# Three attentions turned round: scores by key tiles instead of by query tiles

## The reference

```python
q, k, v = x @ wq, x @ wk, x @ wv                       # [1250, 8, 64]; cross: q of one input, k and v of the other
att = softmax(einsum('bthd,bshd->bhts', q, k) * 64 ** -0.5, axis=-1)
o = einsum('bhts,bshd->bthd', att, v)                  # then an output projection
```

## Time and profile before

| | us |
|---|---|
| median of 3 runs (3291.41 to 3301.77) | 3301.08 |
| profiled execution, whole | 3298.01 |
| profiled execution, span of the instructions | 3296.2 |
| mean granted TensorE clock of the span | 0.949 |
| TensorE matmul busy, share of the span | 2932.8, 89% |
| VectorE busy | 2036.8, 62% |
| ScalarE busy | 1465.3, 44% |
| POOL busy | 940.6, 29% |

### The profile page before, as it was taken

How to read it: one execution, slowest core, us unless ns; L and a number is a source line. 1 busy time by engine, 2 the same in 40 slices (tenths; PEclk the granted TensorE clock), 3 DMA queues, 4 the chain that set the end, 5 groups by cost and what they waited for, 6 DMA issues and landing times. The chain is left out here.

```text
span 3296.2 us, 48091 instructions
## 1 busy us (share of the span) xinstructions
PE 2932.8 (89%) x15718; PEld 2060.1 (62%) x15718; DVE 2036.8 (62%) x4423; ACT 1465.3 (44%) x3160; POOL 940.6 (29%) x994
## 2 busy tenths in 40 slices
PE   5978789999679967699998888989999899998899
PEld 3522277776557644355555765668777687776787
DVE  7989745776421126599996355643777537776444
ACT  1000035666235425477774345533666336664322
POOL 2057663672124431577770000000000000001210
PEclk9999989999779979799999899999999899999999
DMA  3047665331559964554541554136320163311322
GB/s 99 14 134 205 193 165 144 63 61 38 168 164 339 338 195 142 199 154 146 159 122 42 176 132 104 26 107 185 68 59 22 44 189 81 73 25 40 105 83 83
DMA packets 222610, 402.73 MB, mean 122 GB/s; under 512 B 44222, under 2 KB 140626, under 8 KB 218526
## 3 DMA queue, kind: packets, MB, share of 16 engines
q1 hardware_dynamic: 170866, 262.09, 28.0%
q0 software_dynamic: 49744, 134.92, 14.7%
q10 hardware_dynamic: 1756, 2.64, 0.3%
HBM read 315.84 MB, written 87.71 MB: 122 GB/s over the span
## 5 line engine op out<-in xcount | busy, mean ns | idle before, releaser
L904 ACT ACTIVATE at_p<-at_pb,at_max 125x1250 f32<-125x1250 f32 (+4 forms) x320 | 383.8, 1199 | 301.3 <-DVE at_unused L975 272.9
L790 PE MATMUL at_pb<-ident,at_p 125*125 125x125 f32 x2880 | 435.2, 282 | 20.2 <-ACT at_p L904 17.4
L790 PEld LDWEIGHTS at_pb<-ident,at_p 125*125 125x125 f32 x2880 | 392.3, 191 | 82.6 <-ACT at_p L904 23.4
L807 PE MATMUL at_pb<-at_pt,at_v 125*64 125x250 f32 x2880 | 355.3, 383 | 5.2 <-DVE s_t L1008 3.0
L968 DVE TENSOR_REDUCE at_wide<-at_pb 125x1 f32<-125x1024 f32 x240 | 293.6, 1224 | 22.4 <-PE at_pb L773 4.5
L890 ACT ACTIVATE at_pt<-at_pb 125x500 f32<-125x500 f32 (+1 forms) x448 | 232.8, 520 | 97.5 <-PE at_pb L790 93.7
L807 PEld LDWEIGHTS at_pb<-at_pt,at_v 125*64 125x64 f32 x2880 | 188.4, 137 | 103.9 <-issue 13.8
L750 PE MATMUL at_pb<-at_s,at_shared 128*128 128x500 f32 (+1 forms) x1152 | 229.4, 361 | 24.0 <-ACT at_shared L852 24.0
L986 DVE COPY at_pt<-at_pb 125x500 f32<-125x500 f32 (+1 forms) x416 | 232.5, 582 | 22.4 <-PE at_pb L790 22.4
L975 DVE TENSOR_SCALAR_CACHE_REDUCE at_unused<-at_pb,at_wide 125x226 bf16<-125x226 f32 x240 | 107.7, 449 | 205.1 <-PE at_pb L773 202.2
L750 PEld LDWEIGHTS at_pb<-at_s,at_shared 128*128 128x128 f32 x1152 | 195.9, 194 | 57.1 <-ACT at_shared L852 24.7
(11 more groups left out here) (336 smaller groups left out, 5709.2 us busy)
## 6 DMA issues: line engine op xcount, KB each, us to landing
w_ring<-in_L_ffn_w SPq DMA_DIRECT2D x128, 512.0 KB, 12.2
at_shared<-k_parts SPq DMA_DIRECT2D x64, 312.5 KB
ml_w<-in_mlp_w SPq DMA_DIRECT2D x64, 256.0 KB
k_parts<-at_shared SPq DMA_DIRECT2D x64, 250.0 KB, 2.8
q_parts<-at_shared SPq DMA_DIRECT2D x64, 250.0 KB, 3.2
h_edges<-em_both SPq DMA_DIRECT2D x11, 1024.0 KB, 4.1
g_h<-h_edges SPq DMA_DIRECT2D x11, 1024.0 KB, 6.4
at_shared<-q_parts SPq DMA_DIRECT2D x32, 312.5 KB
```

Source lines behind the costliest of these rows:

```text
L790: ins = pe.transpose(pturn[0:TN, g % 2, TN * (t % 4):TN * (t % 4) + TN], p[:, u % 2, TN * t:TN * t + TN], c.ident[0:TN, 0:TN])
L807: ins = pe.matmul(pout[side:side + 64, 0:2 * TN], v[:, t, 2 * j + h, :], p_t[:, q % 2, t, :], start=(t < 2), stop=(t >= keys[u] - 2))
L904: act.activation(p[:, t % 2, 0:w], score[t % 2][0:TN, 0:w], ACT.Exp, bias=neg_max[:, t:t + 1], accum_out=total[:, t:t + 1]).then_inc(exp_d ...
```

## The change

A new function, `attention_by_key`, takes the place of `attention` in the three unmasked attentions; the causal one keeps the old function. The scores are made transposed, 125 keys on the partitions by queries on the columns, so that the exponentials are already in the form that the weighted sum takes and nothing is transposed.

- A *pass* is one head and one half of the queries (16 passes). Its ten *steps* are the key tiles; the half is two chunks of 312 (or 316) columns in two PSUM banks. Two steps are a *stretch* (`u`).
- A step has four score matmuls: high q and low q (stacked on 128 partitions) against high k, then 65 rows: high q against low k, and one row that holds the negative maximum of each query against a row of ones. So the maximum is subtracted by TensorE, and ScalarE's exponential has no bias.
- The maxima come from matmuls of their own, by query tiles of 125 and key pieces of 418 and 416 columns, of the high part of k alone: 15 a pass, three a stretch, in two banks (4 and 5) that the row sums share. VectorE reduces each; the last one of a pass is followed by a small reduction, and SP writes the pass's five columns of maxima as pieces of the row, by five DMAs. The maxima of a pass run six to two stretches ahead of it, those of the first 18 during the v projection.
- The weighted sum: for each step two fp32 matmuls (chunk 0 to partitions 0 to 63, chunk 1 to 64 to 127), summed over ten steps in one of two banks.
- Row sums: POOL adds up the exponentials of some key tiles (five in four additions; three in two in layer 0), VectorE those of the others, and four matmuls with a matrix of ones sum over the partitions. ScalarE copies the sums, spreads a row of 316 over 79 partitions by four by DMA, VectorE inverts them 8 wide, ScalarE sends them to DRAM and spreads them over 64 partitions, and POOL (layer 0: VectorE) multiplies `out_t` in SBUF. The last pass is inverted 316 wide from PSUM and multiplied by VectorE.
- Projections run in the order q, k, v, and SP instead of POOL issues the first pair's loads, in the middle of the second half of k (its q in the second half of q).

```diff
+QUARTERS = ((0, 312), (618, 316))
+MOSTQ = 316
+MAX_CUTS = ((0, 418), (418, 834), (834, N))
...
+        parts = [(kind, half) for kind in "qkv" for half in range(2)]
...
+        pieces_at = {u: [] for u in range(-LEAD, DUOS + 2)}
+        for P in range(PASSES):
+            for k in range(15):
+                pieces_at[NT // 2 * P - LEAD + k // 3].append((P, k // 3, k % 3))
+        sums_at = {NT // 2 * (P + 1) + 1: P for P in range(PASSES)}
...
+        by_pool = [(0, 1), (5,)] if send is not None else [(0, 2), (4,), (6,), (8,)]
+        rest = [t for t in range(NT) if not any(t in g for g in by_pool)]
+        by_dve = [(rest[0], rest[1])] + [(t,) for t in rest[2:]]
...
+                    if x in (begin[1] + 1, begin[3] + 1):
+                        for r in range(RINGS):
+                            sp.wait_ge(stored[r], stores_by(begin[ci], r))
+                        load_pair(sp, 0, kind, first_in)
...
+                for P in range(PASSES):
+                    j, h, half = P // 4, P // 2 % 2, P % 2
+                    sp.wait_ge(max_ready, P + 1)
+                    for i in range(5):
+                        a = 625 * half + TN * i
+                        sp.dma_start(qb[j % 2][h][MAXROW, a:a + TN].bitcast(F32).rearrange("o (p i) -> o p i", p=TN),
+                                     neg[:, P, i:i + 1].bitcast(F32)).then_inc(row_in, 16)
+                    if P % 4 == 0:
+                        if j + 1 < PAIRS_:
+                            if j == 0:
+                                sp.wait_ge(summed, NI)
+                            else:
+                                sp.wait_ge(scored, 4 * NT * j)
+                            load_pair(sp, j + 1, "qk", kq_in[(j + 1) % 2])
...
+                def slot_free(k):
+                    if k >= 2:
+                        if isinstance(user[k - 2], tuple):
+                            pe.wait_ge(freed, pieces_by(k - 2))
+                        else:
+                            pe.wait_ge(sums_out, user[k - 2] + 1)
+                def max_piece(u, m):
+                    P, i, n = pieces_at[u][m]
...
+                    k = slot_of[P, i, n]
...
+                    slot_free(k)
+                    a, b = MAX_CUTS[n]
+                    q0 = TN * (5 * half + i)
+                    pe.matmul(bank[0:TN, 4 + k % 2, 0:b - a], qa[j % 2][h][:, q0:q0 + TN], ka[j % 2][h][:, a:b],
+                              start=True, stop=True).then_inc(filled, 1)
...
+                        if x == first_v:
+                            pe.wait_ge(first_in, 16 * LOADS)
+                            pe.wait_ge(low, first_v)
+                        if x - first_v < LEAD:
+                            for m in range(3):
+                                max_piece(x - first_v - LEAD, m)
...
+                def scores(s):
+                    if t == 0:
+                        pe.wait_ge(row_in, 80 * (P + 1))
...
+                    at = lambda x: bank[0:TN, 2 * ((s + 1) % 2) + x, 0:wide(half)]
+                    for x in range(2):
+                        pe.matmul(at(x), ka[j % 2][h][:, keys], qa[j % 2][h][:, slice(*chunk(half, x))], start=True, stop=False)
+                    for x in range(2):
+                        ins = pe.matmul(at(x), kb[j % 2][h][0:65, keys], qb[j % 2][h][0:65, slice(*chunk(half, x))],
+                                        start=False, stop=True)
+                    ins.then_inc(scored, 1)
...
+                def values(s):
+                    pe.wait_ge(exp_done, s + 1)
+                    for x in range(2):
+                        ins = pe.matmul(bank[64 * x:64 * x + 64, 6 + P % 2, 0:wide(half)], v[:, t, 2 * j + h, :],
+                                        p[:, s % DEEP, x, 0:wide(half)], start=(t == 0), stop=(t == NT - 1))
+                    ins.then_inc(pv_done, 1)
+                def sums(P):
+                    k, w = sum_slot[P], wide(P % 2)
+                    slot_free(k)
+                    pe.wait_ge(dve_added, len(by_dve) * (P + 1))
+                    pe.wait_ge(pool_added, len(by_pool) * (P + 1))
+                    for g in range(2):
+                        for x in range(2):
+                            ins = pe.matmul(bank[64 * x:64 * x + 64, 4 + k % 2, 0:w], ones[:, :], acc[:, P % 2, g, x, 0:w],
+                                            start=(g == 0), stop=(g == 1))
+                    ins.then_inc(filled, 1)
+                for u in range(DUOS + 2):
+                    for m in range(2):
+                        max_piece(u, m)
+                        if u < DUOS:
+                            scores(2 * u + m)
+                    max_piece(u, 2)
+                    if 1 <= u <= DUOS:
+                        values(2 * u - 2)
+                        values(2 * u - 1)
+                    if u in sums_at:
+                        sums(sums_at[u])
...
+                    if t == 2 and 1 <= P <= LAST:
+                        take_values(P - 1)
+                    if t == 3 and 1 <= P <= LAST:
+                        take_sums(P - 1)
+                    if t == 8 and 1 <= P <= LAST:
+                        send_inverse(P - 1)
+                    if t == 1 and 2 <= P <= LAST + 1:
+                        spread_inverse(P - 2)
...
+                    b, w = 2 * ((s + 1) % 2), wide(s // NT % 2)
+                    act.activation(p[:, s % DEEP, :, 0:w], bank[0:TN, b:b + 2, 0:w], ACT.Exp).then_inc(exp_done, 1)
+                    after_exp(s)
...
+                    dve.wait_ge(filled, k + 1)
+                    dve.tensor_reduce(part[:, P, i, n:n + 1], bank[0:TN, 4 + k % 2, 0:MAX_CUTS[n][1] - MAX_CUTS[n][0]],
+                                      AX, ALU.max, negate=True).then_inc(freed, 1)
+                    if (i, n) == (4, 2):
+                        dve.wait_ge(freed, pieces_by(k))
+                        dve.tensor_reduce(neg[:, P, :], part[:, P, :, :], AX, ALU.min).then_inc(max_ready, 1)
...
+                        dve.engine_nop().then_inc(low, 1)
+                        if x - first_v < LEAD:
+                            for m in range(3):
+                                max_piece(x - first_v - LEAD, m)
...
+                for u in range(DUOS + 2):
+                    max_piece(u, 0)
+                    if 1 <= u <= DUOS:
+                        add(2 * u - 2)
+                    max_piece(u, 1)
+                    max_piece(u, 2)
+                    if 1 <= u <= DUOS:
+                        add(2 * u - 1)
+                    P, n = divmod(u, NT // 2)
+                    if n == 3 and 1 <= P <= LAST:
+                        invert(P - 1)
+                    if send is not None and n == 2 and 2 <= P <= LAST:
+                        scale(P - 2)
+                scale_last()
...
-            attention(nc, c, s_t, s_t, s_t, *halves, None, None, scratch, send=(table1, rows1, slots1),
+            attention_by_key(nc, c, s_t, s_t, s_t, *halves, None, None, scratch, send=(table1, rows1, slots1),
...
-                attention(nc, c, s_t, t_t, s_t, zero(whalf(cw, 0)), zero(whalf(cw, 1)), zero(whalf(cw, 2)),
+                attention_by_key(nc, c, s_t, t_t, s_t, zero(whalf(cw, 0)), zero(whalf(cw, 1)), zero(whalf(cw, 2)),
```

More of the change, by code:

```diff
@@ L2437, in program @@
                 normalize(nc, c, x_sb, x_out=x1, keep=keep0, targets=[(s_t, col("ln1_g"), col("ln1_b"))],
-                          next_in=load_first(c, halves[1]))
+                          next_in=load_first(c, halves[0]))
             late0, late1 = ExitStack(), ExitStack()
@@ L2492, in program @@
                           early=all_w(a["tp_w"]), columns=(bcol(a["tv_bcol"]), all_b(a["tp_b"])), after=lambda wo: out_features(
-                              nc, c, t_t, wo, load_first(c, whalf(sw, 1), (bcol(sbr, 0), bcol(sbr, 1)), spatial), residual_d=t_d))
-                attention(nc, c, s_t, s_t, s_t, whalf(sw, 0), whalf(sw, 1), whalf(sw, 2), bcol(sbr, 0), bcol(sbr, 1), scratch,
+                              nc, c, t_t, wo, load_first(c, whalf(sw, 0), (bcol(sbr, 0), bcol(sbr, 1)), spatial), residual_d=t_d))
+                attention_by_key(nc, c, s_t, s_t, s_t, whalf(sw, 0), whalf(sw, 1), whalf(sw, 2), bcol(sbr, 0), bcol(sbr, 1), scratch,
                           pick=spatial, early=all_w(a["sp_out_w"]), ahead=True, columns=(bcol(sbr, 2), all_b(a["sp_out_b"])),
                           after=lambda wo: out_features(nc, c, s_t, wo, load_first(
-                              c, zero(whalf(cw, 1)), (zerob(bcol(cbr, 0)), zerob(bcol(cbr, 1))))))
+                              c, zero(whalf(cw, 0)), (zerob(bcol(cbr, 0)), zerob(bcol(cbr, 1))))))
                 def out1(wo):
```

418 lines of the change are left out of this document (added).

## The result

The changed kernel takes 3443.76 us (3440.61 to 3446.37) against 3300.07: a ratio of 1.0435, interval 1.0423 to 1.0448. It is slower by 143 us where 20 was forecast, and outside the range. The profiled execution took 3446.37 us, its span 3444.6.

What follows compares the result with a forecast made beforehand. TensorE was taken to bound the kernel: its loop and drain fall from 298 to 270 us, but waits add +17 us in the first attention and +1 in the others, +18 together: 3316, taken as 3320 us, range 3244 to 3372.

Steps and rivals of the forecast that it cites:

- What TensorE streams: Unmasked attention loops: a two-tile stretch takes 3.15 us; loop and drain take 270 us against 298.
- (1) V projection: Maxima share two banks, so TensorE stands 1.84 us at each of six V items, 11 us.
- (2) First keys: First pair's key loads, now SP's in the K projection: TensorE waits 2 to 3 us; 0 to 6.
- (3) Rows: Start of each pass: five row DMAs, last issued 1.4 us in, landing 2.2 us, arrive just in time.
- Rival E: Rows land in 3.4 us, so each of 36 passes loses 1.2 us: 3363 us; chance 0.23.
- (3) Rows behind the loads: Row DMAs queue behind the next pair's loads on SP: 6 us, then 2.1 us twice; 10 us an attention.
- The inverse chain: Two small DMAs and a broadcast after the row sums: has a pass, 17 us, for itself.
- Clock: After an idle stretch TensorE runs at a granted clock of 0.50 for 3 us, 1.5 us lost.
- (4) Additions: VectorE's additions meeting POOL's delay a maximum's bank: 3 us an attention, 0 to 15; 8 us in the first.
- Rival D: VectorE's four additions a pass each wait out a whole POOL addition, VectorE sets the pace: 3362 us; chance 0.10.
- The first attention: With 160 indirect DMAs, slower loads and fuller VectorE: 315 us against 297.7, +17 us.

Runs made afterwards that it cites:

- the kernel with five, five and two: Next pair's twelve loads issued five, five and two over three passes, against four each, atop maxima two stretches earlier and V-projection maxima spaced out: 3252.80 us, ratio 0.9856.

## Why the prediction was wrong, step by step

- *What TensorE streams*: right. A stretch 3.13 us (3.15), the row sums 1.05, a pass without waits 16.7 to 16.9 us in the second and third attention (16.8). The gain in streaming is real: in the kernel with five, five and two the second attention's loop and drain take 269 us (270; 298 before).
- *(1) V projection*: right. 1.77 us at each of six items (1.84).
- *(2) First keys*: right. 2.4, 3.1 and 7.4 us (3, 3 and 5).
- *(3) Rows*: the step that failed first, a term of the sum that was mis-sized. "Five issues at 0.34 us, the last 1.4 us in" took a duration of other small DMAs; these take 0.675 us each, and the last starts 2.9 us in. With 2.1 us of landing that is 5.0 us where 3.6 were at hand. Rival E's outcome came, rows late in nearly every pass, but not by the landing that E named: the landing was right (2.1 to 2.3 us, 2.2 forecast), the issue was not. It cost 68 us by the run with early maxima and some 84 counted in the passes other than 0, 4 and 8 (87 less the 3 of moved maxima), against 43 in E and none in the forecast. The forecast did see that this decides, and took its value without a row for an issue of this shape. On the landing, the Trainium skill ("DMA: Bandwidth & Descriptors", section "Why small descriptors are slow (HBM only)") spares transfers within SBUF the penalty of small pieces. The trace goes with it as far as it reaches: pieces of 4 bytes within SBUF took 2.1 us, pieces of 8 bytes to DRAM 3.4; no run changes the destination alone.
- *(3) Rows behind the loads*: right for pass 0 (6.7 us, 6 forecast), and wrong for the others, because of a sentence elsewhere: "The inverse chain ... has a pass, 17 us, for itself." In the code `sums(P - 1)` stands at stretch 1 of a pass and `invert(P - 1)` at stretch 3, in VectorE's order ahead of maxima: two stretches, 6.3 us. I priced the chain on an empty DMA queue and let only the rows meet the loads, as they share SP's queue. But the sums, on ScalarE's queue, met them too, and VectorE waited for them 6.3 to 7.2 us in four of the six passes 4 and 8; in the other two their issues held ScalarE. The loads cost some 70 us by the runs (3375.82 to 3306.37), and 17 more when spread better, against 44 forecast with the colder stretches.
- *Clock*: the mechanism right (1.5 us a time), the count wrong: it comes in most passes of the first attention, not in two or three.
- *(4) Additions*: small, as taken, in the second and third attention: with early maxima and spread loads TensorE waits 2.1 us for VectorE in the second one's loop (3 forecast), and 9.4 in the first one's (8 forecast). Where they meet, VectorE's 0.80 us become up to 2.10, which is the rest of POOL's addition (1.41 us) and most of its own. The Trainium skill ("SBUF — State Buffer", section "SBUF: two separate sides") has the loser blocked until the other ends. This trace agrees, and the earlier trace rows too: the subtraction that took 1.91 us began with 1.11 us left of a POOL addition that the rows do not show (3091.34, 1.59 us long), and "0.97" was the rest of that addition, not a milder effect. Rival D did not come about, though they do meet: in the changed kernel 32 of the second attention's 64 additions on VectorE take over 1.2 us, but none of the 64 over 1.97, and all together 72 us where D had 154; VectorE is busy 198 of the 316 us and sets no pace.
- *The first attention* lost the most (71 us) for the same two reasons: its rows are ready later (a quiet last stretch is 2.3 us too long, not 1.3), and after ten of its waits the next stretch takes 4.1 us or more at a lower clock. Its sum also has a slip that changes little: the terms of its 18 us (6 + 2.1 x 2, and 2 us more for each of three loads) add up to 16.2.
- What stays open: how the loads' cost divides among VectorE's reciprocal, POOL's multiplication and ScalarE's issues: the run with the late inverse shows the first and bares the others, but none takes them away one by one.

## What to carry to other kernels

A wait in an in-order engine is priced by the slack between producer and consumer in the written order, counted in stretches of the code, and by what stands behind it; write both down for every DMA that closes a loop, however small. A burst of loads delayed small DMAs on both issuing queues here, and some of their issues: spread it over the time that it has, or keep small DMAs with readers out of its 19 us. And where a term has no margin, take its duration from a row of the same shape or price it as late.

## What the runs showed of the hardware

- A DMA of 125 pieces of 4 bytes from 125 partitions into one row of SBUF takes 0.675 us to issue, and reaches its reader 2.1 to 2.3 us after the issue began; one of 158 pieces of 16 bytes to DRAM takes 0.23 to 0.34 us to issue.
- With twelve loads of 312.5 KB under way, a small DMA on another queue reached its reader 13 us after its issue began, and in two of six passes an issue took 3.5 and 4.1 us instead of 0.78 (the row sums', least/median/greatest):

```profile
L1466 ACTq DMA_DIRECT2D ak_total<-ak_sums x90: 601/782/4075, 571.7 to 3138.9; - x90
```

- An addition of two SBUF tiles on VectorE that began while POOL was adding took the rest of POOL's addition and 0.7 us more: 2.10 us with 1.41 us left, 1.30 us with 0.62 left, against 0.80 alone.
